# Sliding-window attention layers: the causal mask and the query lengths move from TensorE and a separate scaling pass into the VectorE pass over the scores; scaled rotary tables are kept in DRAM

## The chip, the cores and the metric

One core of one Trainium2 chip runs the whole program in one launch. The metric is the device time of an execution in microseconds, as the median of several runs. A profiled execution gives the trace that is read below; it has its own time.

## The reference

The input is x of 4 sequences of 2048 tokens with 256 features, in fp32. First comes a full attention block (16 heads of 16) with a Gaussian prior on the scores. Then come two layers of local attention and feed-forward. Only the local attention is touched in substance by the change. It computes, with windows of 128 tokens and 8 heads of 64:

```python
h = shift_token(x); q, k, v = split(h @ wqkv)      # 256 -> 3 x 512
q = q / max(|q|, 1e-12) * q_scale                  # the same for k
q, k = rotary_xpos(q, k)                           # q*cos*s + rotate_half(q)*sin*s, k with 1/s
sim = 8 * q @ k.T                                  # 128 queries by 256 keys: window before and own
sim = where((i < j) | (i > j + 128) | (j == -1), -max, sim)
x = x + (softmax(sim) @ v) @ wo
```

A length of q is one factor for each query and head, and so one factor for each row of `sim`.

## The kernel before, in words

`program` (the last function but one) runs `attention`, and then for each of two layers `local_layer` and `feed_forward`. x stays in SBUF as `xs`, 64 tiles of 128 tokens.

`local_layer` handles the 64 tiles one after another (NT = 64; each sequence has W = 16 of them). Every engine has its own written-out order, a loop over iterations n, and works in iteration n on several tiles at once: the projections of tile n, the transposes of q and k of tile n-1, the scores of tile n-2, transposes of probabilities and P V of tile n-3, and the output projection of tile n-4. Semaphores tie the engines together. The order in one iteration is:

- TensorE: `qkv` for q and k (12 matmuls of 512 columns, L1039), transpose of q (`qk_T`, L1050), `qkv` for v (6 matmuls), scores of head pair 0 (`sim`), transposes of p for pairs 0 and 1 (L1080), transpose of k, scores of pair 1, output projection (L1103, L1106), scores of pair 2, transposes of p for pairs 2 and 3, transpose of x for the next tile (L1024), scores of pair 3, P V (L1092). A `sim` is a bf16 matmul of the mask against an identity over a whole bank (L1061), which starts the bank, then two matmuls with `kh` and two with `kl` that add the scores (L1068). q and k are fp32 numbers split in a high and a low part.
- VectorE: `scale` of tile n-1 (L1265: q and k together, 1024 elements a partition, times their inverse lengths), a reciprocal, `o_lo` (L1295), `rotate` (L1242, 1024 elements), low part of q, first half of `rotate_half` (L1248), maximum of the scores of pair 0 (`sim`, L1282: one reduce for two heads, negated), second half of `rotate_half`, low part of k, maximum of pair 1, `lengths` (L1256, L1258), a reciprocal, maximum of pair 2, residual add `out` (L1303, L1305), a reciprocal, `x_lo` (L1232, the low part of the next tile's input), maximum of pair 3, a reciprocal.
- ScalarE: copies out of PSUM, squares, and the exponentials `sim` (L1181), which take the negated maximum as bias and write the sum of each row. In its order, `x_hi` (L1140), which `x_lo` needs, stands behind the exponentials of pair 2.
- GpSimd: a memset at one n in 16 (`zero_row`, L1356), `normalise` of four pairs (L1375, 512 elements each), `scale_table` (L1361: the rotary table of the next tile times q_scale and k_scale), and its part of `lengths`: the sum of the two rotation products (L1366) and the inverse lengths (L1368, a power of -0.5).
- SyncE issues the DMAs: `stack` (L1414 to L1418) moves q and k parts into place for the scores, `load_table` (L1402) fetches a table of 128 KB for every tile. For tile t of each of the 4 sequences the same 16 tables are fetched and scaled again.

The score banks are `S[0]` and `S[1]`, used alternately, so pair 2 waits for the exponentials of pair 0 and pair 3 for those of pair 1.

Of the kernel before, what the change touches and what calls it, by code (L numbers as in the profile page):

```python
# [257 lines left out]
def attention(nc, xs, x1, a):  # L258
# [297 lines left out]
    def vector(eng):  # L556
# [67 lines left out]
        def pass1(n, c):  # L624
            g, qb = divmod(n + LEAD, W)
            if g >= NB * HA:
                return
            i, k = slot["p1", g, qb, c]
            dve.wait_ge(s_full[i], k)
            o = 512 * c - 128 * qb  # L630
            if -512 - BAND < o < 128 + BAND:
                if junk_of:
                    dve.wait_ge(*junk_of.pop())
                junk_of.append((s_free[i], k))
                t = eng.tensor_tensor_reduce(junk[:, :], banks[i], gw[:, o + WIDE0:o + WIDE0 + 512], 1.0, 0.0, ALU.add, ALU.max, mx[g % 2][:, qb, c:c + 1])  # L635
            else:
                t = eng.tensor_reduce(mx[g % 2][:, qb, c:c + 1], banks[i], X, ALU.max)  # L637
            t.then_inc(s_free[i], 1)
            if (qb, c) == (W - 1, 3):
                dve.wait_ge(s_free[i], k)  # L640
                dve.wait_ge(s_dve, step.on(eng.tensor_reduce(nm[:, :], mx[g % 2][:, :, :], X, ALU.max, negate=True)))
                if g:
                    i, k = slot["rows", g - 1]
                    dve.wait_ge(s_full[i], k)
                dve.wait_ge(s_dve, step.on(eng.tensor_copy(pk[:, 0, :], nm[:, :])))
                dve.wait_ge(s_dve, step.on(eng.tensor_tensor(r1[:, :], nm[:, :], pk[:, 0, :], ALU.subtract)))
                dve.wait_ge(s_dve, step.on(eng.tensor_copy(pk[:, 1, :], r1[:, :])))
                eng.tensor_tensor(pk[:, 2, :], r1[:, :], pk[:, 1, :], ALU.subtract).then_inc(s_pk, 1)
# [264 lines left out]
NEG = -3.3895313892515355e38  # L913
# [5 lines left out]
def rotary():  # L919

    half = np.arange(0, DL, 2, dtype=np.float32)
    inv = np.float32(1.0) / np.float32(10000.0) ** (half / np.float32(DL))
    t = np.arange(L, dtype=np.float32)
    f = t[:, None] * inv[None, :]
    f = np.concatenate([f, f], 1)
    base = (half + np.float32(0.4 * DL)) / np.float32(1.4 * DL)
    power = (t - np.float32(L // 2)) / np.float32(64.0)
    s = base[None, :] ** power[:, None]
    s = np.concatenate([s, s], 1)
    sign = np.concatenate([-np.ones(32), np.ones(32)]).astype(np.float32)  # L930
# [24 lines left out]
def local_layer(nc, xs, layer, a):  # L955
# [6 lines left out]
    ident, identb = sb("ident", [128, 128]), sb("identb", [128, 128], BF16)  # L962
    mask = [sb(f"mask{i}", [128, 2, 2, 128], BF16) for i in range(2)]
# [7 lines left out]
    ss, ri = [sb(f"ss{i}", [128, 16]) for i in range(2)], [sb(f"ri{i}", [128, 16]) for i in range(2)]  # L971
# [7 lines left out]
    oT = [sb(f"oT{k}", [128, 512], F32R) for k in range(2)]  # L979
    G = [ph.ps(f"G{i}", [128, 512]) for i in range(2)]  # L980
# [31 lines left out]
    def tensor(eng):  # L1012
# [30 lines left out]
        def qk_T(t, n):  # L1043
            pe.wait_ge(s_ready, t + 1)
            if n:
                pe.wait_ge(s_ql, t + 1)
            elif t:
                pe.wait_ge(s_kl, t)
            for i in range(4):
                m = eng.transpose(T[:, i * 128:i * 128 + 128], t1[t % 2][:, n, 2 * i:2 * i + 2, :].rearrange("p h d -> p (h d)"), ident[:, :])  # L1050
            m.then_inc(s_qkT, 1)

        def sim(t, pair):
            w, s = t % W, S[pair % 2]
# [6 lines left out]
            eng.matmul(s[:, :], identb[:, :], mask[place(t, 0)][:, :, :, :].rearrange("p h k n -> p (h k n)"), start=True, stop=False, skip_group_check=True)  # L1061
# [71 lines left out]
    def scalar(eng):  # L1133
# [37 lines left out]
        def sim(t, pair):  # L1171
# [5 lines left out]
            for h in range(2):  # L1177
# [3 lines left out]
                y = eng.activation(dst, src, ACT.Exp, bias=nm[t % 2][:, hh:hh + 1], accum_out=sm[t % 2][:, hh:hh + 1])  # L1181
# [44 lines left out]
    def vector(eng):  # L1226
# [33 lines left out]
        def scale(t):  # L1260
            s = t % 2
# [3 lines left out]
            eng.tensor_tensor(flat, flat, ri[s][:, :].unsqueeze(2).to_broadcast([128, 16, DL]), ALU.mult).then_inc(s_ready, 1)  # L1265
# [12 lines left out]
        def sim(t, pair):  # L1278
# [3 lines left out]
            eng.tensor_reduce(nm[t % 2][:, 2 * pair:2 * pair + 2], s[:, :].rearrange("p (h k) -> p h k", h=2) if w else z[:, :, 1, :],  # L1282
                              X, ALU.max, negate=True).then_inc(s_max, 1)

        def recip(t, pair):
            o = 2 * pair
            dve.wait_ge(s_exp, pos(t, pair))
            if t > 1:
                dve.wait_ge(s_norm, pos(t - 2, pair))
            eng.reciprocal(rc[t % 2][:, o:o + 2], sm[t % 2][:, o:o + 2]).then_inc(s_rc, 1)  # L1290
# [30 lines left out]
        for n in range(NT + 4):  # L1321
            if n == 0:
                dve.wait_ge(s_cw, 48)
                for i in range(2):
                    for k in range(2):
                        m = eng.tensor_copy(mask[i][:, :, k, :], mask32.rearrange("p (h k n) -> p h k n", h=2, k=2)[:, :, k ^ i, :])
# [4 lines left out]
            on(recip, n - 3, 3)  # L1331
# [9 lines left out]
            on(recip, n - 2, 0)  # L1341
            on(sim, n - 2, 2)
            on(out, n - 4)
            on(recip, n - 2, 1)
            on(x_lo, n + 1)
            on(sim, n - 2, 3)
            on(recip, n - 2, 2)

    def gpsimd(eng):
# [13 lines left out]
        def lengths(t):  # L1363
# [4 lines left out]
            eng.tensor_tensor(ri[s][:, :], ss[s][:, :], nh[:, :], ALU.pow).then_inc(s_inv, 1)  # L1368

        def normalise(t, pair):  # L1370
# [3 lines left out]
            pool.wait_ge(s_rc, pos(t, pair))  # L1374
# [10 lines left out]
        for n in range(NT + 4):  # L1385
# [4 lines left out]
            on(scale_table, n + 1)  # L1390
            on(lengths, n)

    def sync(eng):
# [36 lines left out]
        load_wqkv(2)  # L1430
        for n in range(NT + 1):
# [345 lines left out]
```

## Time and profile before

| | |
|---|---|
| median of 3 runs | 6263.26 us (6263.15 to 6264.88) |
| the profiled execution's own time | 6266.61 us |
| its span | 6264.8 us |
| local layers, by the windows 3595 to 4450 and 4936 to 5792 | 855 and 856 us |
| busy in the first of them | PE 831.16, DVE 750.74, ACT 642.51, POOL 761.39 us |

PE is TensorE's matmuls, PEld its weight loads, DVE VectorE, ACT ScalarE, POOL GpSimd, SPq the queue of SyncE. A row of a timeline gives the start in us from the span's start, the duration in us, engine, line, operation, output tile <- input tiles, shape and count; "x2" is two instructions run together into one row, and a bracket at the end is idle time before it and who ended it. Starts tell more than durations here: on TensorE and VectorE an instruction starts before the record of the one ahead of it has ended, so the price of one is read from start to start.

### The profile page before, as it was taken

To read this page: it belongs to the slowest core of one execution; us is meant where nothing else is said; L and a number is where in the kernel's file an instruction comes from. 1 tells how busy PE (TensorE), PEld (TensorE's weight loads), DVE (VectorE), ACT (ScalarE), POOL (GpSimd) and SP (SyncE) were. 2 spreads that over 40 slices of the span, in tenths; PEclk is the share of its full clock that TensorE was granted. 3 is DMA by queue.
4 is the path that set the end of the run, shared out by engine and by line. 5 is a ranking of instruction groups with operands and counts; after the bars stand their busy time and mean duration, and the time that the engine had idled before them with its cause. 6 is when DMAs were issued, how large, how long until landed. Compare 5 with 4: busy or idle time off the path is not lost. (4 is left out here: it accounts for less than half of the span.)

```text
span 6264.8 us, 108066 instructions
## 1 busy us (share of the span) xinstructions
PE 5943.0 (95%) x40672; PEld 3318.7 (53%) x40672; DVE 4985.5 (80%) x10559; ACT 3827.3 (61%) x6354; POOL 1850.8 (30%) x1259
## 2 busy tenths in 40 slices
PE   6999999999998999999999799999899899999999
PEld 2333333333333333332323278888788688888788
DVE  5877888888888777888888588898666688888666
ACT  1666665666665666656666567777533477777332
POOL 3001000000000011000000089899400399989111
PEclk7999999999999999999999999999999899999999
DMA  2001101001001111001000145445300245544211
GB/s 84 23 28 35 32 16 43 27 29 31 28 20 38 33 35 35 17 30 29 17 16 16 43 108 117 112 114 114 78 11 8 67 112 117 117 113 111 61 51 44
DMA packets 264079, 338.39 MB, mean 54 GB/s; under 512 B 47324, under 2 KB 166916, under 8 KB 263556
## 3 DMA queue, kind: packets, MB, share of 16 engines
q1 hardware_dynamic: 263556, 331.48, 21.0%
q8 instruction: 321, 5.26, 0.4%
q14 instruction: 202, 1.65, 0.1%
HBM read 104.04 MB, written 41.94 MB: 23 GB/s over the span
## 5 line engine op out<-in xcount | busy, mean ns | idle before, releaser
L533 ACT ACTIVATE a_pr<-a_w 128x1024 f32<-128x1024 f32 x2048 | 2076.7, 1023 | 1150.5 <-PE a_w L421 830.1
L637 DVE TENSOR_REDUCE a_mx<-a_b 128x1 f32<-128x512 f32 x2688 | 1740.0, 685 | 327.7 <-PE a_b L405 308.5
L405 PE MATMUL a_b<-a_kp,a_qp 96*128 96x512 bf16 x4096 | 1445.6, 387 | 111.8 <-DVE a_mx L637 48.6
L421 PE MATMUL a_w<-a_qp,a_kp 99*128 99x512 bf16 x4096 | 1226.1, 380 | 33.8 <-ACT a_pr L533 33.7
L635 DVE CUSTOM_DVE_ANT_0 a_junk<-a_b,a_gw 128x512 bf16<-128x512 f32 x1408 | 965.5, 686 | 248.7 <-PE a_b L405 209.2
L452 PE MATMUL a_po<-a_pr,a_v 128*17 128x512 f32 x8192 | 1068.9, 595 | 0.5 <-ACT a_pr L533 0.5
L405 PEld LDWEIGHTS a_b<-a_kp,a_qp 96*128 96x128 bf16 x4096 | 335.4, 97 | 1255.9 <-issue 701.6
L1375 POOL TENSOR_TENSOR l_p<-l_p,l_rc 128x512 f32<-128x512 f32 (+1 forms) x512 | 725.4, 1445 | 28.7 <-DVE l_rc L1290 28.5
L421 PEld LDWEIGHTS a_w<-a_qp,a_kp 99*128 99x128 bf16 x4096 | 388.4, 98 | 521.7 <-ACT a_pr L533 110.8
L1039 PE MATMUL l_G<-l_wqkv,l_hT 128*128 128x512 f32 x2304 | 620.8, 415 | 40.4 <-DVE l_hT L1232 24.0
L746 POOL TENSOR_TENSOR a_rs<-a_ve,a_nh 128x2 f32<-128x2 f32 (+1 forms) x48 | 38.4, 800 | 2015.6 <-DVE a_ve L613 1752.5
L1181 ACT ACTIVATE l_p<-l_S,l_nm 128x256 f32<-128x256 f32 (+1 forms) x1024 | 470.6, 469 | 209.5 <-DVE l_nm L1282 209.4
L1514 PE MATMUL f_F<-f_hT,f_w 128*114 128x512 f32 x2304 | 560.5, 399 | 0.7 <-DVE f_b L1647 0.7
L1039 PEld LDWEIGHTS l_G<-l_wqkv,l_hT 128*128 128x128 f32 x2304 | 426.2, 194 | 148.9 <-DVE l_hT L1232 31.8
L756 POOL TENSOR_TENSOR a_less<-a_tmp,a_stage 128x512 f32<-128x512 f32 x64 | 74.1, 1158 | 1324.4 <-ACT a_tmp L525 880.0
L1514 PEld LDWEIGHTS f_F<-f_hT,f_w 128*114 128x114 f32 x2304 | 401.7, 177 | 120.2 <-issue 0.8
L1368 POOL TENSOR_TENSOR l_ri<-l_ss,l_nh 128x16 f32<-128x16 f32 x128 | 372.5, 2910 | 22.1 <-DVE l_ss L1258 14.3
L1366 POOL TENSOR_TENSOR l_t<-l_t 128x1024 f32<-128x1024 f32 x128 | 305.3, 2385 | 155.7 <-DVE l_t L1248 155.7
L1282 DVE TENSOR_REDUCE l_nm<-l_S 128x2 f32<-128x512 f32 (+1 forms) x512 | 338.1, 660 | 11.0 <-PE l_S L1068 10.8
L1569 ACT ACTIVATE f_u<-f_uf 114x512 fp32r<-114x512 f32 x192 | 121.4, 632 | 368.0 <-DVE f_uf L1621 368.0
L436 PEld LDWEIGHTS a_w<-a_mt,a_sel 96*32 96x32 bf16 x4864 | 111.1, 93 | 417.0 <-issue 417.0
L1189 ACT ACTIVATE l_pT<-l_R 128x512 f32<-128x512 f32 (+1 forms) x512 | 271.5, 583 | 77.4 <-PE l_R L1080 70.6
(167 smaller groups left out, 8465.6 us busy)
## 6 DMA issues: line engine op xcount, KB each, us to landing
l_qs<-l_qT SPq DMA_DIRECT2D x512, 128.0 KB, 2.3
l_kh<-l_kT SPq DMA_DIRECT2D x512, 128.0 KB, 2.4
l_kl<-l_kT SPq DMA_DIRECT2D x256, 128.0 KB, 2.4
a_qp<-q_parts SPq DMA_DIRECT2D x384, 64.0 KB, 2.2
a_kp<-k_parts SPq DMA_DIRECT2D x384, 64.0 KB, 2.2
a_xc<-in_x SPq DMA_DIRECT2D x32, 512.0 KB
l_tab<-in_rotary SPq DMA_DIRECT2D x128, 128.0 KB, 2.4
q_parts<-a_stage SPq DMA_DIRECT2D x32, 384.0 KB, 2.5
```

The lines of the kernel that those rows point to most:

```text
L405: eng.matmul(bk, qp[s][0:96, qb * 128:qb * 128 + 128], kp[s][0:96, c * 512:c * 512 + 512], start=True, stop=True).then_inc(full, 1)
L421: m = eng.matmul(wide[u][:, c * 512:c * 512 + 512], kp[s][0:99, kb * 128:kb * 128 + 128], qp[s][0:99, u * 1024 + c * 512:u * 1024 + c * 51 ...
L452: m = eng.matmul(po[32 * j:32 * j + DA + 1, :], v[b % 2][:, kb, h, :], pr[(2 * n + j // 2) % NP][:, (j % 2) * 512:(j % 2) * 512 + 512], st ...
L533: eng.activation(pr[(2 * n + u) % NP][:, :], wide[u][:, :], ACT.Exp, scale=0.25).then_inc(s_exp[u], 1)
L635: t = eng.tensor_tensor_reduce(junk[:, :], banks[i], gw[:, o + WIDE0:o + WIDE0 + 512], 1.0, 0.0, ALU.add, ALU.max, mx[g % 2][:, qb, c:c + 1])
L637: t = eng.tensor_reduce(mx[g % 2][:, qb, c:c + 1], banks[i], X, ALU.max)
L1039: m = eng.matmul(G[n % 2][:, :], hT[x][:, c * 128:c * 128 + 128], wq[z][:, c, n * 512:n * 512 + 512], start=i == 0, stop=i == 5)
L1181: y = eng.activation(dst, src, ACT.Exp, bias=nm[t % 2][:, hh:hh + 1], accum_out=sm[t % 2][:, hh:hh + 1])
L1282: eng.tensor_reduce(nm[t % 2][:, 2 * pair:2 * pair + 2], s[:, :].rearrange("p (h k) -> p h k", h=2) if w else z[:, :, 1, :], X, ALU.max, n ...
L1368: eng.tensor_tensor(ri[s][:, :], ss[s][:, :], nh[:, :], ALU.pow).then_inc(s_inv, 1)
L1375: eng.tensor_tensor(z, z, rc[t % 2][:, o:o + 2].unsqueeze(2).to_broadcast([128, 2, 256 if w else 128]), ALU.mult).then_inc(s_norm, 1)
L1514: m = eng.matmul(f[0:FW, :], w1[x][:, c, col * FW:col * FW + FW], hT[g % 2][z][:, c, :], start=n == 0, stop=n == 5)
```

## The change

The mask matmul goes, and with it the bf16 identity. The first `kh` matmul of a pair now starts the bank. The table of q is negated (factor -8), so the scores come out negated and unscaled by the length of q. VectorE's `sim` becomes two `tensor_tensor_reduce` a pair, one for each head: (score + mask) times the inverse length of q, written back in place in PSUM, with the minimum into `nm`. Its mask is 0 or a huge positive number. The exponential reads the bank with scale -1. `scale` is left with k alone (512 elements), and the transpose of q waits for the rotation instead of for `scale`. There are three `ri` buffers instead of two, with two waits on GpSimd for them. The four reciprocals of a tile become two of double width. Scaled tables are written to DRAM during the first 16 tiles of a layer (`keep_table`) and fetched from there for the other 48, for which `scale_table` is not run. In `attention` the start value of an existing `tensor_tensor_reduce` becomes the lowest number instead of 0.

```diff
 def sim(t, pair):                       # tensor
-    pe.wait_ge(s_idb, 1)
-    pe.wait_ge(s_mask, 1)
-    eng.matmul(s[:, :], identb[:, :], mask[place(t, 0)]..., start=True, stop=False, skip_group_check=True)
...
-                       start=False, stop=True, skip_group_check=True)
+                       start=x is kh and h == 0, stop=True, skip_group_check=True)

 def qk_T(t, n):                         # tensor
-    pe.wait_ge(s_ready, t + 1)
+    pe.wait_ge(s_ready if n else s_rot, t + 1)

 def scale(t):                           # vector
-    flat = t1[s][:, :, :, :].rearrange("p a h d -> p (a h) d")
-    eng.tensor_tensor(flat, flat, ri[s][:, :]....to_broadcast([128, 16, DL]), ALU.mult).then_inc(s_ready, 1)
+    k = t1[t % 2][:, 1, :, :]
+    eng.tensor_tensor(k, k, ri[t % 3][:, HL:2 * HL]....to_broadcast([128, HL, DL]), ALU.mult).then_inc(s_ready, 1)

 def sim(t, pair):                       # vector
     dve.wait_ge(s_sim, pos(t, pair))
-    eng.tensor_reduce(nm[t % 2][:, 2 * pair:2 * pair + 2], s..., X, ALU.max, negate=True).then_inc(s_max, 1)
+    dve.wait_ge(s_inv, t + 1)
+    for h in range(2):
+        hh = 2 * pair + h
+        y = s[:, h * 256:h * 256 + 256] if w else z[:, h, 1, :]
+        m = eng.tensor_tensor_reduce(y, y, mask[place(t, 0)][:, :] if w else mask[0][:, 128:256], ri[t % 3][:, hh:hh + 1], -LOWEST,
+                                     ALU.add, ALU.min, nm[t % 2][:, hh:hh + 1])
+    m.then_inc(s_max, 1)

-def recip(t, pair):                     # 2 elements; after exp of the pair
+def recip(t, half):                     # 4 elements; after exp of pair 2 * half + 1
...
 def lengths(t):                         # gpsimd
+    if t > 2:
+        pool.wait_ge(s_max, pos(t - 3, 3))
+        pool.wait_ge(s_ready, t - 2)
     eng.tensor_tensor(ri[t % 3][:, :], ss[s][:, :], nh[:, :], ALU.pow).then_inc(s_inv, 1)
...
-            on(scale_table, n + 1)
+            if n + 1 < W:
+                scale_table(n + 1)

 def load_table(t):                      # sync
+    for k in range(max(t - 3, 0), t - 2) if t < W else range(W - 3, W):
+        sp.wait_ge(s_kept[k % 3], 16 * (k // 3 + 1))
-    eng.dma_start(tab[t % 3]..., a["rotary"][:, t % W, :, :, :])...
+    eng.dma_start(tab[t % 3]..., a["rotary"][:, t, :, :, :] if t < W else scaled[t % W, :, :, :, :])...
+def keep_table(t):
+    sp.wait_ge(s_table, t + 1)
+    eng.dma_start(scaled[t, :, :, :, :], tab[t % 3]...).then_inc(s_kept[t % 3], 16)
```

In VectorE's order the reciprocal of pairs 0 and 1 stands behind the residual add, and that of pairs 2 and 3 behind `scale` of the next iteration.

## Rows read from the trace of the kernel before

**Rows 1.** The page's busy times: us, share of the span, instructions.
```profile
PE 5943.0 (95%) x40672; PEld 3318.7 (53%) x40672; DVE 4985.5 (80%) x10559; ACT 3827.3 (61%) x6354; POOL 1850.8 (30%) x1259
```
**Rows 2.** Windows: us, busy (count) of PE, PEld, DVE, ACT, POOL, clock, DMA.
```profile
5200.00:5400.00 200.00, 198.38 (x1544) 173.03 (x1546) 179.01 (x300) 154.53 (x420) 184.58 (x107) 1.00 0.51 115
```
**Rows 3.** Timeline of PE, two tile starts, a pair's scores, a later tile start.
```profile
4111.68 3.06 PE L1039 MATMUL l_G<-l_wqkv,l_hT 128*128 128x512 f32 x12
...
4124.98 3.06 PE L1039 MATMUL l_G<-l_wqkv,l_hT 128*128 128x512 f32 x12
...
4212.99 0.38 PE L1061 MATMUL l_S<-l_mask,l_identb 128*128 128x512 bf16 x1
...
4213.44 0.40 PE L1068 MATMUL l_S<-l_kl,l_qs 128*128 128x256 f32 x2
4213.68 1.08 PE L1103 MATMUL l_G<-l_wo,l_oT 128*128 128x512 f32 x4
...
4219.54 3.06 PE L1039 MATMUL l_G<-l_wqkv,l_hT 128*128 128x512 f32 x12
```
**Rows 4.** Timeline of POOL in the same stretches.
```profile
4109.11 2.91 POOL L1368 TENSOR_TENSOR l_ri<-l_ss,l_nh 128x16 f32<-128x16 f32 x1 [0.15 <-DVE l_ss L1258]
...
4122.35 2.91 POOL L1368 TENSOR_TENSOR l_ri<-l_ss,l_nh 128x16 f32<-128x16 f32 x1
...
4178.33 3.03 POOL L1375 TENSOR_TENSOR l_p<-l_p,l_rc 128x512 f32<-128x512 f32 x3
...
4206.22 6.00 POOL L1375 TENSOR_TENSOR l_p<-l_p,l_rc 128x512 f32<-128x512 f32 x4
4212.18 1.18 POOL L1361 TENSOR_TENSOR l_tab<-l_tab,l_qsc 128x256 f32<-128x256 f32 x1
4214.04 2.39 POOL L1366 TENSOR_TENSOR l_t<-l_t 128x1024 f32<-128x1024 f32 x1 [0.69 <-DVE l_t L1248]
4216.63 2.91 POOL L1368 TENSOR_TENSOR l_ri<-l_ss,l_nh 128x16 f32<-128x16 f32 x1 [0.20 <-DVE l_ss L1258]
```
**Rows 5.** Timeline of DVE in the same stretches.
```profile
4178.33 4.11 DVE L1265 TENSOR_TENSOR l_t<-l_t,l_ri 128x1024 f32<-128x1024 f32 x1
...
4206.43 1.91 DVE L1265 TENSOR_TENSOR l_t<-l_t,l_ri 128x1024 f32<-128x1024 f32 x1
...
4209.98 1.34 DVE L1242 TENSOR_TENSOR l_t<-l_qk,l_tab 128x1024 f32<-128x1024 f32 x1 [0.98 <-ACT l_qk L1148]
...
4212.69 0.68 DVE L1282 TENSOR_REDUCE l_nm<-l_S 128x2 f32<-128x512 f32 x1
...
4217.57 0.42 DVE L1305 TENSOR_TENSOR xs<-l_G,xs 128x256 f32<-128x256 f32 x1
4217.91 0.16 DVE L1290 RECIPROCAL l_rc<-l_sm 128x2 f32<-128x2 f32 x1
4218.71 0.42 DVE L1232 TENSOR_TENSOR l_hT<-l_G,l_hT 128x256 fp32r<-128x256 f32 x1 [0.64 <-ACT l_hT L1140]
```
**Rows 6.** Lines L1265 and L1248 over the span: duration ns minimum/median/maximum.
```profile
L1265 DVE TENSOR_TENSOR l_t<-l_t,l_ri x128: 1226/1985/4115, 3608.2 to 5786.4; 128x1024 f32<-128x1024 f32 x128
...
L1248 DVE TENSOR_TENSOR l_t<-l_qk,l_tab x256: 673/681/928, 3601.3 to 5780.1; 128x512 f32<-128x512 f32 x128
```
**Rows 7.** Timeline of DVE in the attention block: reduces and `tensor_tensor_reduce`, 512 wide.
```profile
1999.33 1.28 DVE L637 TENSOR_REDUCE a_mx<-a_b 128x1 f32<-128x512 f32 x2
...
2002.20 0.08 DVE L635 DVE_READ_ACCUMULATOR2_ANT a_mx<- 128x1 f32 x1
2002.43 0.69 DVE L635 CUSTOM_DVE_ANT_0 a_junk<-a_b,a_gw 128x512 bf16<-128x512 f32 x1
2003.05 0.08 DVE L635 DVE_READ_ACCUMULATOR2_ANT a_mx<- 128x1 f32 x1
2003.05 0.69 DVE L637 TENSOR_REDUCE a_mx<-a_b 128x1 f32<-128x512 f32 x1
```
**Rows 8.** Timeline of SPq: the load of a table.
```profile
4205.23 0.58 SPq L1402 DMA_DIRECT2D l_tab<-in_rotary  x1
```

More of the change, by code:

```diff
@@ L17 @@
 EPS = 1e-5
+LOWEST = -3.4028234663852886e38
 HA, DA = 16, 16
@@ L634, in pass1 @@
                 junk_of.append((s_free[i], k))
-                t = eng.tensor_tensor_reduce(junk[:, :], banks[i], gw[:, o + WIDE0:o + WIDE0 + 512], 1.0, 0.0, ALU.add, ALU.max, mx[g % 2][:, qb, c:c + 1])
+                t = eng.tensor_tensor_reduce(junk[:, :], banks[i], gw[:, o + WIDE0:o + WIDE0 + 512], 1.0, LOWEST, ALU.add, ALU.max, mx[g % 2][:, qb, c:c + 1])
             else:
@@ L912 @@
 HL, DL = 8, 64
-NEG = -3.3895313892515355e38
+FAR = 3.3895313892515355e38
 FC, FW = 6, 114
@@ L961, in local_layer @@
     qsc = sb("qsc", [128, 2, 2, DL])
-    ident, identb = sb("ident", [128, 128]), sb("identb", [128, 128], BF16)
-    mask = [sb(f"mask{i}", [128, 2, 2, 128], BF16) for i in range(2)]
+    ident = sb("ident", [128, 128])
+    mask = [sb(f"mask{i}", [128, 256], BF16) for i in range(2)]
     nh = sb("nh", [128, 16])
@@ L970, in local_layer @@
     t2 = sb("t2", [128, 2, HL, DL])
-    ss, ri = [sb(f"ss{i}", [128, 16]) for i in range(2)], [sb(f"ri{i}", [128, 16]) for i in range(2)]
+    ss, ri = [sb(f"ss{i}", [128, 16]) for i in range(2)], [sb(f"ri{i}", [128, 16]) for i in range(3)]
     qT, kT = [sb(f"qT{k}", [128, 4, 128], F32R) for k in range(2)], [sb(f"kT{k}", [128, 4, 128], F32R) for k in range(2)]
@@ L979, in local_layer @@
     oT = [sb(f"oT{k}", [128, 512], F32R) for k in range(2)]
+    scaled = nc.dram_tensor(f"scaled{layer}", [W, 128, 2, 2, DL], F32, kind="Internal").ap()
     G = [ph.ps(f"G{i}", [128, 512]) for i in range(2)]
@@ L1180, in sim @@
                 src = s[:, h * 256:h * 256 + 256] if w else z[:, h, 1, :]
-                y = eng.activation(dst, src, ACT.Exp, bias=nm[t % 2][:, hh:hh + 1], accum_out=sm[t % 2][:, hh:hh + 1])
+                y = eng.activation(dst, src, ACT.Exp, scale=-1.0, bias=nm[t % 2][:, hh:hh + 1], accum_out=sm[t % 2][:, hh:hh + 1])
             y.then_inc(s_exp, 1)
@@ L1281, in sim @@
             dve.wait_ge(s_sim, pos(t, pair))
-            eng.tensor_reduce(nm[t % 2][:, 2 * pair:2 * pair + 2], s[:, :].rearrange("p (h k) -> p h k", h=2) if w else z[:, :, 1, :],
-                              X, ALU.max, negate=True).then_inc(s_max, 1)
-        def recip(t, pair):
-            o = 2 * pair
-            dve.wait_ge(s_exp, pos(t, pair))
+            dve.wait_ge(s_inv, t + 1)
[6 more added lines that the diff above has]
+        def recip(t, half):
+            o = 4 * half
+            dve.wait_ge(s_exp, pos(t, 2 * half + 1))
             if t > 1:
-                dve.wait_ge(s_norm, pos(t - 2, pair))
-            eng.reciprocal(rc[t % 2][:, o:o + 2], sm[t % 2][:, o:o + 2]).then_inc(s_rc, 1)
+                dve.wait_ge(s_norm, pos(t - 2, 2 * half + 1))
+            eng.reciprocal(rc[t % 2][:, o:o + 4], sm[t % 2][:, o:o + 4]).then_inc(s_rc, 1)
         def o_lo(t):
@@ L1430, in sync @@
         load_wqkv(2)
+        keep_table(0)
         for n in range(NT + 1):
@@ L1439, in sync @@
                 stack(n - 1, 1)
+            if n + 1 < W:
+                keep_table(n + 1)
             if n + 2 < NT:
```

35 lines of the change are left out of this document (17 added, 18 removed).

## The prediction, made before the changed kernel was run

> **What bounds the kernel now.** I read the page's busy times first: PE is the busiest engine, at 95% [rows 1]. The windows then show that in a local layer PE is busy for 198.38 of 200 us at full clock, and that POOL (184.58) and DVE (179.01) stand close behind [rows 2]. PE's timeline gives the period: the projections of one tile start at 4111.68 and those of the next at 4124.98, 13.30 us later [rows 3]. The PE order is a solid chain with no hole worth a tenth. The two layers hold 128 such tiles.
>
> What matters is how far the next limits are. POOL's inverse lengths in the same two tiles start at 4109.11 and 4122.35, 13.24 us apart [rows 4]: POOL and DVE drift ahead of PE, by 0.06 a tile, so they turn in a loop of their own of 13.24. That loop is seen in the timelines of POOL and DVE from 4206 on [rows 4, 5]. When the power (L1368) ends, POOL begins to normalise. Three normalisations alone take 3.03 us, but four beside DVE's work take 6.00 instead of 4.0 [rows 4]. The two missing microseconds are `scale` and `rotate`: `scale` takes 1.23 when nothing stands beside it and 1.91 to 1.99 here [rows 5, 6], and `rotate` ends only once a normalisation has ended. Operations of DVE with two SBUF inputs and those of POOL take turns, whole instruction by whole instruction. So the loop is: power, two normalisations with `scale` between them, a third, `rotate`, low part, first half of the rotation, maximum 0 (4212.69), the other half, low part, maximum 1, lengths, power (4216.63, 2.91 long), normalise at 4219.5.
>
> The Trainium skill has this in "SBUF — State Buffer" (the part on ports and contention): the pair of ports that VectorE and GpSimd share is an exclusive lock for a whole instruction, taken by VectorE operations with two SBUF inputs. The 6.00 against 4.0 agrees. It also says that a pass with one input in PSUM does not take the lock, so the new passes over the scores should not be stretched.
>
> A third chain goes through `x_lo`: projections, copy of q and k, `rotate`, three maxima, the exponentials of pair 2, `x_hi`, `x_lo` (4218.71, 0.42 long), projections of the next tile at 4219.54. It has 0.41 us of air less the hand-over, so it is about 12.9 long [rows 3, 5].
>
> **PE.** The mask matmul starts at 4212.99, the `kl` pair at 4213.44 and what follows at 4213.68 [rows 3]. Two 256-column matmuls cost 0.24, `kh` the same, and the mask 0.45 - 0.24 = 0.21. Four a tile are 0.84, which leaves PE a floor of 13.30 - 0.84 = 12.46. The bounds of one are 0.16 (the first `kh` weights no longer load behind the mask) and 0.23. If PE alone counted, the layers would win 0.84 x 128 = 108 us. It does not: the loop of 13.24 takes over after 0.06.
>
> **DVE, `scale`.** 512 elements instead of 1024. Alone the sizes take 1.23 and 0.68 [rows 6], so 0.55 less, both on DVE and in the time POOL stands still. This is in the POOL loop. It is not in the `x_lo` chain: DVE is idle for 0.98 before `rotate`, until ACT's copy [rows 5].
>
> **DVE, the scores.** One reduce has a start-to-start price of 0.60 (two are 1.28, the last 0.68) [rows 7]. Two passes of 256 replace it. The nearest row for 256 elements out of PSUM is the residual add: 4217.57 to 4217.91, 0.34 [rows 5]. Two are 0.68, so a pair costs d = +0.08. Each pass also carries a read of its accumulator. A reduce behind it starts in the same instant (both 2003.05), but another such pass starts 0.23 after the read (2002.20 to 2002.43); there a semaphore for the junk buffer lies between [rows 7], which the new code does not have. So d lies between +0.08 and 0.34 + 0.23 + 0.34 - 0.60 = +0.31, and if the gap follows both passes, at +0.54. Below 0.08 I see nothing. Writing back to PSUM in place has no row, nor the factor read per partition; the residual add reads PSUM and writes SBUF, and so does the attention pass; 512 against 256 elements (0.60 against 0.34) is 1.0 ns an element. I take d = 0.12, nearest to the add, with something for the read in the middle.
>
> The Trainium skill speaks against splitting here: "VectorE: DVE Perf Modes", section "The DRAIN you can't avoid", has the next operation start only once the pipe is empty, and a fixed 151 cycles beside one cycle an element. By that rule two passes of 256 are 0.85 against 0.69, d = +0.16. The rows show starts 0.08 before the end of the one ahead; by the rule instead of the rows the total would be some 10 us higher than mine.
>
> **The loops after.** POOL loop: 13.24 - 0.55 + 2d (maxima 0 and 1 lie in it; maximum 2 does not) = 12.69 + 2d = 12.93. `x_lo` chain: 12.9, less a reciprocal moved out from ahead of maximum 2 (0.08), plus 3d, less 0.1 to 0.2 because PE brings the transposes of p earlier and ACT, which stands between maxima 1 and 2, no longer waits for them: 13.0 to 13.1. PE: 12.46. I take a period of 13.0: 0.30 less, in 128 tiles 38.4 us.
>
> **The slip.** One tile in 16 has a memset ahead of the normalisation. `scale` and the normalisation then start together (both 4178.33), POOL wins three times, and `scale` takes 4.11 [rows 4, 5]. That is 2.1 over its usual 1.99, of which the idle 0.98 covers most of one microsecond: 1.2 lost. After the change the third normalisation needs the reciprocal that stands behind `scale` on DVE, so `scale` starves behind two at most: 2.0 + 0.7 = 2.7, covered by the idle time. It happened six times: 7.2 us.
>
> **What costs nothing, and why.** `scale_table` (1.18) goes from 48 tiles in 64, but POOL waits 0.69 for DVE right behind it [rows 4]: the wait becomes 1.9. POOL busy falls by about 1.1 x 96 = 100 us, and the time by nothing; it would count only if POOL were loaded without gaps. Two of four reciprocals go, 0.08 each from start to start: one is the 0.08 above, the other lies ahead of idle time. The transpose of q no longer waits for `scale`; PE gets to it some 2.9 into the tile, so this is air. POOL's two new waits stand ahead of the power, on maxima and a `scale` more than a tile old; behind them only the normalisations queue. DVE's new wait for the inverse lengths is for a tile whose power ended a period earlier. SP: `keep_table` waits for a table that POOL has scaled at 4213.4, halfway in its tile, and SP gets there at about 4205.23, a microsecond before the next tile starts on PE [rows 8]; behind it stand only a table two tiles ahead and the next `stack`, over six microseconds later. One issue of 0.6 fits. Once a layer, ahead of table 16, SP waits for a 128 KB store to land, some 2 to 3 us, inside the same gap. 32 stores in all. The start value in attention is another constant: nothing. With PE at 12.4 of 13.0 I expect its clock to stay at 2.4 GHz in the layers; the rows of before cannot show it.
>
> **Sum.** The profiled execution took 6266.6. 6266.6 - 38.4 - 7.2 = 6221.0. The median shown is 3.3 below that execution, so 6217.7, as 6218.
>
> **Rivals.**
> - *The accumulator gap is real.* With d = 0.31 the POOL loop is 13.31 and the `x_lo` chain 13.3 to 13.5: the period is what it was, only the slip pays, 6256 to 6270. For it: the 0.23 in [rows 7]. Against: a self-wait explains part of it.
> - *DVE's passes become the bound and the kernel slows.* If each pass pays its gap, or reading and writing one PSUM bank in place is slower than the add, d reaches 0.54: the loop is 13.77, 0.47 over 13.30, in 128 tiles +60, less 7: 6316. In between, d = 0.40 gives 13.49, +24 - 7 = 6280. The point is d = 0.30, where 12.69 + 2d passes 13.30. For it: DVE and POOL were 0.06 from binding already, so almost nothing has to go wrong. Against: no row shows a pass of DVE over PSUM that takes more than that 1.0 ns an element.
> - *The locks fall well.* If, with `scale` short, `rotate` finds POOL idle, another microsecond leaves the loop, and PE's floor binds: 6266.6 - 108 - 7 - 3 = 6148. Against: four normalisations and half a `scale` need 4.6 us from the power's end and `rotate` starts 3.7 into the tile; they must meet.
> - *It doesn't do what it says*, for instance tables from DRAM come late: the load is issued two tiles ahead, so hardly.
>
> **How the numbers follow.** Forecast (d from 0.08 to 0.22, period 12.85 to 13.13, 6200 to 6236) 0.57; partial gap and accumulator gap, 6236 to 6275, 0.20; slower by over 0.2%, 0.17; PE's floor 0.05; the last 0.01. About 0.2% (12.5 us) is what a measurement of this kernel tells from no change. Faster by more (below 6250.8): 0.57 + 0.05 + 0.05 of the partial gap = 0.67. Same: 0.14. Slower (above 6275.8): 0.19 with the tail of the gap case. The range for 8 in 10 leaves out most of the PE floor and the upper half of the slower cases: 6188 to 6284.
>
> **What would show it.** PE: no L1061, its floor visible as idle time of about 0.5 a tile. Starts of L1368 12.9 to 13.1 apart. `scale` near 1.3 to 1.5 us and POOL's four normalisations 5.5 instead of 6.0. Two custom passes whose starts lie 0.34 to 0.38 apart; 0.57 would be the gap. POOL waiting about 1.9 ahead of L1366 from tile 16 on. No `scale` of 4 us. The prediction is wrong if the pair costs over 0.90, or if `rotate` no longer meets a normalisation.

## The result, and the profile after

| | before | after |
|---|---|---|
| median | 6263.2 us (4 runs) | 6310.66 us (4 runs, 6308.54 to 6311.41) |
| the profiled execution | 6266.61 us | 6308.54 us |

The ratio is 1.0076, with a 95% interval of 1.0058 to 1.0093: slower, by 47 us. The forecast was 6218.

The windows of the same stretch as [rows 2] show that PE did give up its load (188.74 of 200 us busy instead of 198.38), and POOL too (139.46 instead of 184.58). DVE's share is about the same.

```profile
5200.00:5400.00 200.00, 188.74 (x1423) 160.56 (x1422) 176.91 (x433) 151.85 (x408) 139.46 (x89) 1.00 0.46 109
```

PE's timeline has the next tile's projections 13.88 after those of the last (4217.46 to 4231.34; 13.30 before, [rows 3]). Now they wait for `x_lo` (L1231). The `kh` matmuls of a pair start at 4222.20, `kl` at 4222.44 and what follows at 4222.67, so 0.47 instead of the 0.69 from 4212.99 to 4213.68 in [rows 3]: the mask's 0.22 is saved in full.

```profile
4217.46 3.07 PE L1041 MATMUL l_G<-l_wqkv,l_hT 128*128 128x512 f32 x12 [0.24 <-DVE l_hT L1231]
...
4222.20 0.39 PE L1067 MATMUL l_S<-l_kh,l_qs 128*128 128x256 f32 x2
4222.44 0.40 PE L1067 MATMUL l_S<-l_kl,l_qs 128*128 128x256 f32 x2
4222.67 1.04 PE L1079 MATMUL l_R<-l_ident,l_p 128*128 128x128 f32 x8
...
4231.34 1.90 PE L1041 MATMUL l_G<-l_wqkv,l_hT 128*128 128x512 f32 x7 [0.23 <-DVE l_hT L1231]
```

DVE's timeline of that tile answers to [rows 5]:

```profile
4218.13 1.18 DVE L1266 TENSOR_TENSOR l_t<-l_t,l_ri 128x512 f32<-128x512 f32 x1
...
4221.20 2.09 DVE L1244 TENSOR_TENSOR l_t<-l_qk,l_tab 128x1024 f32<-128x1024 f32 x1 [0.66 <-ACT l_qk L1147]
...
4224.41 0.48 DVE L1287 CUSTOM_DVE_ANT_0 l_S<-l_S,l_mask,l_ri 128x256 f32<-128x256 f32 x1
4224.81 0.14 DVE L1287 DVE_READ_ACCUMULATOR2_ANT l_nm<- 128x1 f32 x1
4224.81 0.48 DVE L1287 CUSTOM_DVE_ANT_0 l_S<-l_S,l_mask,l_ri 128x256 f32<-128x256 f32 x1
4225.22 0.14 DVE L1287 DVE_READ_ACCUMULATOR2_ANT l_nm<- 128x1 f32 x1
4225.22 0.68 DVE L1250 TENSOR_TENSOR l_t<-l_qk,l_tab 128x512 f32<-128x512 f32 x1
```

Two things are to be seen. A pair costs 0.81 from start to start (4224.41 to 4225.22), so d = 0.81 - 0.60 = 0.21; the forecast took 0.12. And `rotate` lasts 2.09 instead of 1.34. POOL's timeline says why (the first row is a window that begins inside the four normalisations, so it holds the last two):

```profile
4220.17 2.04 POOL L1381 TENSOR_TENSOR l_p<-l_p,l_rc 128x512 f32<-128x512 f32 x2
...
4217.73 4.48 POOL L1381 TENSOR_TENSOR l_p<-l_p,l_rc 128x512 f32<-128x512 f32 x4
4225.98 2.38 POOL L1369 TENSOR_TENSOR l_t<-l_t 128x1024 f32<-128x1024 f32 x1 [3.77 <-DVE l_t L1250]
4228.73 2.91 POOL L1374 TENSOR_TENSOR l_ri<-l_ss,l_nh 128x16 f32<-128x16 f32 x1 [0.36 <-DVE l_ss L1260]
```

The last two normalisations take 2.04 from 4220.17, so the last one starts at about 4221.17, and `rotate` asks at 4221.20. It loses by 0.03 and stands until POOL is done at 4222.21; it ends 1.08 after that. In the kernel before, `rotate` asked while the third was running (4209.98, the third from 4209.20 to 4210.23) and went ahead of the last. Over all tiles the median of `rotate` went from 1459 to 2094 ns:

```profile
L1244 DVE TENSOR_TENSOR l_t<-l_qk,l_tab x128: 1224/2094/2099, 3593.4 to 5820.9; 128x1024 f32<-128x1024 f32 x128
```

### The profile page after: what moved, and what is told of

Same layout as the page of the kernel before. It is cut to its first block and busy times, and to the rows that moved or that the text cites. A ratio compares the mean times of both kernels' runs of the same rounds, so it can differ in the third digit from the quotient of the medians.

```text
span 6306.8 us, 108286 instructions
## 1 busy us (share of the span) xinstructions
PE 5905.7 (94%) x40160; PEld 3257.2 (52%) x40160; DVE 5022.6 (80%) x11837; ACT 3843.6 (61%) x6354; POOL 1588.6 (25%) x1163
## 5 line engine op out<-in xcount | busy, mean ns | idle before, releaser
L1381 POOL TENSOR_TENSOR l_p<-l_p,l_rc 128x512 f32<-128x512 f32 (+1 forms) x512 | 562.2, 1126 | 23.6 <-DVE l_rc L1296 23.2
L1287 DVE CUSTOM_DVE_ANT_0 l_S<-l_S,l_mask,l_ri 128x256 f32<-128x256 f32 (+1 forms) x1024 | 444.9, 474 | 7.5 <-PE l_S L1067 7.4
L1244 DVE TENSOR_TENSOR l_t<-l_qk,l_tab 128x1024 f32<-128x1024 f32 x128 | 252.6, 1973 | 93.7 <-ACT l_qk L1147 92.9
```

Source lines behind the costliest of these rows:

```text
L1287: m = eng.tensor_tensor_reduce(y, y, mask[place(t, 0)][:, :] if w else mask[0][:, 128:256], ri[t % 3][:, hh:hh + 1], -LOWEST, ALU.add, ALU ...
L1381: eng.tensor_tensor(z, z, rc[t % 2][:, o:o + 2].unsqueeze(2).to_broadcast([128, 2, 256 if w else 128]), ALU.mult).then_inc(s_norm, 1)
```

## The experiments

Each starts from the changed kernel, or where it says so from the kernel before. Medians are of 4 or 10 executions (e6 has one), the ratio is to the kernel before, executed beside them. Periods are read from the starts of the projections on PE. Theory A, in what was expected, is that the order in which `rotate` and the last normalisation get the lock sets the period; theory B, that the longer passes over the scores do it alone.

**e1: the last normalisation after `rotate`.**

```diff
             for pair in range(4):
+                if pair == 3 and n < NT:
+                    pool.wait_ge(s_turn, n + 1)      # incremented by rotate(n)
                 on(normalise, n - 3, pair)
```

> The changed kernel; only edit: POOL normalises pair 3 of tile n-3 only after DVE's rotate of tile n. Theory A (the shared lock: with the half-size scale, normalisation 3 starts in the same instant as rotate, 4221.20, and rotate runs 2.10 instead of 1.34): rotate goes back to about 1.35; normalisation 3 then meets the first rotate_half instead, so maximum 0 starts some 0.35 earlier in the tile, period 13.5 instead of 13.88, about 6265 us. Theory B (the longer passes over the scores alone set the period, the lock is incidental): period stays within 0.1 of 13.88, 6300 to 6315.

Measured: 6273.98 us, ratio 1.0014 (1.0005 to 1.0024). DVE's, POOL's and PE's timelines:

```profile
4212.26 1.23 DVE L1244 TENSOR_TENSOR l_t<-l_qk,l_tab 128x1024 f32<-128x1024 f32 x1 [0.66 <-ACT l_qk L1147]
...
4214.01 1.15 DVE L1250 TENSOR_TENSOR l_t<-l_qk,l_tab 128x512 f32<-128x512 f32 x1
```
```profile
4213.57 1.04 POOL L1381 TENSOR_TENSOR l_p<-l_p,l_rc 128x512 f32<-128x512 f32 x1 [1.29 <-DVE l_t L1244]
```
```profile
4208.53 3.06 PE L1041 MATMUL l_G<-l_wqkv,l_hT 128*128 128x512 f32 x12 [0.24 <-DVE l_hT L1231]
...
4222.02 3.07 PE L1041 MATMUL l_G<-l_wqkv,l_hT 128*128 128x512 f32 x12 [0.23 <-DVE l_hT L1231]
```

One added wait on an engine with air takes 37 us off. `rotate` is back at 1.23, the normalisation now meets the first `rotate_half` (1.15 instead of 0.68), and the period is 13.49, as theory A had it.

**e2: the last normalisation after the first `rotate_half`.** As e1, but the semaphore is incremented by `rotate_half(n, 0)`.

> The changed kernel; only edit: POOL normalises pair 3 of tile n-3 only after the first rotate_half of tile n. Theory A: rotate about 1.25 to 1.35 and the first rotate_half 0.68, maximum 0 about 0.75 earlier in the tile; the second rotate_half may wait up to 0.3 for normalisation 3; period 13.1 to 13.3, 6210 to 6240. Theory B: unchanged or slower, because POOL now waits more: 6300 to 6330.

Measured: 6256.75 us, ratio 0.9986 (0.9977 to 0.9996). The tile starts are 13.28 apart:

```profile
4206.32 3.07 PE L1041 MATMUL l_G<-l_wqkv,l_hT 128*128 128x512 f32 x12 [0.24 <-DVE l_hT L1231]
...
4219.60 3.07 PE L1041 MATMUL l_G<-l_wqkv,l_hT 128*128 128x512 f32 x12 [0.24 <-DVE l_hT L1231]
```

`rotate` and the first `rotate_half` are free now, and the second `rotate_half` is held for 0.26:

```profile
4210.06 1.23 DVE L1244 TENSOR_TENSOR l_t<-l_qk,l_tab 128x1024 f32<-128x1024 f32 x1 [0.66 <-ACT l_qk L1147]
...
4213.21 0.94 DVE L1250 TENSOR_TENSOR l_t<-l_qk,l_tab 128x512 f32<-128x512 f32 x1
```

The period is inside what theory A gave, the total 17 us above it. Part of that, some 5 us, is that the first 15 tiles of a layer, in which POOL still scales tables, ran at 13.50; I had not reckoned with them. The rest was not looked into.

**e3: `scale` on 1024 elements again.** The length of q is applied twice.

```diff
-            k = t1[t % 2][:, 1, :, :]
-            eng.tensor_tensor(k, k, ri[t % 3][:, HL:2 * HL]...)
+            k = t1[t % 2][:, :, :, :].rearrange("p a h d -> p (a h) d")
+            eng.tensor_tensor(k, k, ri[t % 3][:, :]...)
...
-            pe.wait_ge(s_ready if n else s_rot, t + 1)
+            pe.wait_ge(s_ready, t + 1)
```

> The changed kernel, with scale on 1024 elements again (q and k), and the transpose of q waiting for it as before; the length of q is then applied twice, so the scores are not the reference's. Theory A: 0.5 us more of DVE work a tile pushes normalisation 3 behind rotate, rotate 1.4 to 1.6, period 13.65, about 6282: faster than the changed kernel with more work on the engine. Theory B: DVE has 0.5 to 0.7 more a tile, period 13.9 to 14.4, 6312 to 6375.

Measured: 6298.25 us, ratio 1.0054 (1.0039 to 1.0069). DVE does more and the kernel is 12 us faster than the changed one. The two ratios alone hardly tell that from nothing; the tile starts do, 13.67 apart instead of 13.88. `rotate` takes 1.62, and the first `rotate_half` 0.93:

```profile
4207.85 0.93 DVE L1250 TENSOR_TENSOR l_t<-l_qk,l_tab 128x512 f32<-128x512 f32 x1
...
4216.30 1.71 DVE L1266 TENSOR_TENSOR l_t<-l_t,l_ri 128x1024 f32<-128x1024 f32 x1
...
4219.37 1.62 DVE L1244 TENSOR_TENSOR l_t<-l_qk,l_tab 128x1024 f32<-128x1024 f32 x1 [0.66 <-ACT l_qk L1147]
```

The sign and the period (13.67) are theory A's; the total is 16 us above its number.

**e4: the kernel before without the mask matmul**, the first `kh` matmul starting the bank, nothing in its place.

```diff
-            eng.matmul(s[:, :], identb[:, :], mask[place(t, 0)]..., start=True, stop=False, skip_group_check=True)
...
-                                   start=False, stop=True, skip_group_check=True)
+                                   start=x is kh and h == 0, stop=True, skip_group_check=True)
```

> The kernel before without the mask matmul and nothing in its place (the softmax runs over all 256 keys). Theory A, with the loop of POOL and DVE at 13.24: period 13.2 to 13.25, 6250 to 6257. Rival (PE alone bounds the kernel before): period 12.46, about 6155.

Measured: 6256.18 us, ratio 0.9985 (0.9976 to 0.9995). Tile starts are 13.25 apart:

```profile
4214.63 3.07 PE L1039 MATMUL l_G<-l_wqkv,l_hT 128*128 128x512 f32 x12
...
4227.88 3.06 PE L1039 MATMUL l_G<-l_wqkv,l_hT 128*128 128x512 f32 x12
```

So of PE's 0.84 only 0.05 a tile was to be had: the loop of 13.24 read from [rows 4] is real.

**e5: one pass of 512 for two heads**, with the factor and the minimum of one head for both; the first window of a sequence keeps two.

```diff
-            for h in range(2):
+            for h in range(1 if w else 2):
                 hh = 2 * pair + h
-                y = s[:, h * 256:h * 256 + 256] if w else z[:, h, 1, :]
+                y = s[:, :] if w else z[:, h, 1, :]              # the mask tile is 512 wide
```

> The changed kernel with one pass of 512 for the two heads of a pair instead of two of 256 (both heads then share the factor and the minimum of one head; the first window of a sequence keeps two passes), so the output is not the reference's. In the changed kernel the pair costs 0.81 from start to start, 0.21 over the reduce. Theory A (price and lock together): one pass costs 0.60 to 0.66, the cost over the reduce falls to about 0.05; the chain through x_lo gets 0.45 to 0.5 shorter, so tiles start earlier against POOL, normalisation 3 comes behind rotate again (rotate 1.3 to 1.8); period 12.9 to 13.2, 6210 to 6245. Rival (the price counts, the lock doesn't flip): period 13.88 - 0.48 = 13.4, about 6255 to 6265, rotate still 2.1.

Measured: 6201.19 us, ratio 0.9897 (0.9880 to 0.9913). From start to start the pass is 0.67 (d = 0.07), and `rotate` is held in 6 of 128 tiles only:

```profile
4213.39 1.23 DVE L1244 TENSOR_TENSOR l_t<-l_qk,l_tab 128x1024 f32<-128x1024 f32 x1 [0.80 <-ACT l_qk L1147]
...
4215.99 0.75 DVE L1287 CUSTOM_DVE_ANT_0 l_S<-l_S,l_mask,l_ri 128x512 f32<-128x512 f32 x1
4216.66 0.14 DVE L1287 DVE_READ_ACCUMULATOR2_ANT l_nm<- 128x1 f32 x1
4216.66 0.68 DVE L1250 TENSOR_TENSOR l_t<-l_qk,l_tab 128x512 f32<-128x512 f32 x1
```

The period is 12.86, and it and the time are even just below theory A's ranges. 0.14 less a pair took 1.02 off the tile; the price alone, in three or four pairs, would have taken 0.4 to 0.6.

**e6: the factor as the constant 1.0** in the passes; the lengths of q are left out.

```diff
-                m = eng.tensor_tensor_reduce(y, y, mask..., ri[t % 3][:, hh:hh + 1], -LOWEST,
+                m = eng.tensor_tensor_reduce(y, y, mask..., 1.0, -LOWEST,
```

> The changed kernel with the factor of the passes over the scores as the constant 1.0 instead of the inverse length of q (left out, so the scores are too large). One look at a pass's price, 0.40 from start to start and 0.48 long against 0.34 and 0.42 of the residual add of the same size. If the factor read per partition is the surplus: 0.34 to 0.36 and 0.42. If it is the write back to PSUM or the accumulator read: 0.40 as before, and the period 13.88.

Measured: 6216.53 us in one execution. A pair is 0.72 (4219.72 to 4220.44, d = 0.12), and `rotate` isn't held:

```profile
4217.13 1.22 DVE L1244 TENSOR_TENSOR l_t<-l_qk,l_tab 128x1024 f32<-128x1024 f32 x1 [0.74 <-ACT l_qk L1147]
...
4218.87 0.93 DVE L1250 TENSOR_TENSOR l_t<-l_qk,l_tab 128x512 f32<-128x512 f32 x1
4219.72 0.42 DVE L1287 CUSTOM_DVE_ANT_0 l_S<-l_S,l_mask 128x256 f32<-128x256 f32 x1
4220.06 0.14 DVE L1287 DVE_READ_ACCUMULATOR2_ANT l_nm<- 128x1 f32 x1
4220.06 0.46 DVE L1287 CUSTOM_DVE_ANT_0 l_S<-l_S,l_mask 128x256 f32<-128x256 f32 x1
4220.44 0.14 DVE L1287 DVE_READ_ACCUMULATOR2_ANT l_nm<- 128x1 f32 x1
4220.44 0.68 DVE L1250 TENSOR_TENSOR l_t<-l_qk,l_tab 128x512 f32<-128x512 f32 x1
```

The factor read per partition is the surplus: without it the first pass is 0.34, exactly the residual add. The second is 0.38; I put its 0.04 down to the read of the accumulator ahead of it, which no run separates. This kernel has, by accident, the d of the forecast, and it has the period of the forecast: 13.02 against 13.0. Its one execution took 6216.5 us, against 6221.0 in the forecast's sum for a profiled execution. The 0.09 a pair between it and the changed kernel are worth 0.86 a tile.

**e7: the passes write to SBUF.** In this cut `d` is the tile that is written, and not the price d.

```diff
+            if t > 1:
+                dve.wait_ge(s_pT, 4 * (t - 2) + pair + 1)        # the p tile has been read
...
-                m = eng.tensor_tensor_reduce(y, y, mask...
+                m = eng.tensor_tensor_reduce(d, y, mask...       # d: this head's rows of the p tile
...
-                y = eng.activation(dst, src, ACT.Exp, scale=-1.0, ...
+                y = eng.activation(dst, dst, ACT.Exp, scale=-1.0, ...
```

> The changed kernel with the passes writing to the p tile in SBUF, where the exponential works in place, instead of back into the score bank. If the write to PSUM is the surplus of 0.06 a pass: 0.34 to 0.36 from start to start, six passes in the x_lo chain give 0.35, period about 13.5. If it isn't: 0.40, and the period moves only by what the exponentials cost out of SBUF (0.47 from start to end now): 13.8 to 14.2.

Measured: 6312.61 us, ratio 1.0075 (1.0060 to 1.0090). The passes still start 0.40 and 0.41 apart, and the period is 13.88. The write back in place costs nothing:

```profile
4213.71 0.47 DVE L1290 CUSTOM_DVE_ANT_0 l_p<-l_S,l_mask,l_ri 128x256 f32<-128x256 f32 x1
4214.11 0.08 DVE L1290 DVE_READ_ACCUMULATOR2_ANT l_nm<- 128x1 f32 x1
4214.11 0.47 DVE L1290 CUSTOM_DVE_ANT_0 l_p<-l_S,l_mask,l_ri 128x256 f32<-128x256 f32 x1
```

**e8: the kept tables alone, in the kernel before** (the hunks of `scale_table`, `load_table`, `keep_table` and `rotate` of the change, nothing else).

> The kernel before with one part of the change alone: scaled tables kept in DRAM, scale_table run for 16 tiles of 64. All theories: POOL busy 100 us less, the first rotate_half 0.68 instead of 0.92 from tile 16 on, period still 13.29 because PE sets it: 6260 to 6268. A gain of over 10 us would mean that POOL's load as such mattered.

Measured: 6259.39 us, ratio 0.9991 (0.9981 to 1.0000), period still 13.29, and POOL busy 101 us less in the windows of the two layers. That is 6 us at most. One part of what was expected did not come: the first `rotate_half` stays at 0.92. So in this kernel it is the last normalisation that holds it, and not `scale_table`.

**e9: a mask matmul back in the changed kernel**, its result overwritten by the next.

```diff
+            eng.matmul(s[:, :]..., mask[0][:, 0:128], mask[0][:, :].unsqueeze(1).to_broadcast([128, 2, 256]), start=True, stop=False, ...)
             pe.wait_ge(s_qs[t % 2], 64 * (t // 2 + 1))
```

> The changed kernel with a bf16 matmul of 512 columns back in front of the kh matmuls of every pair, whose result the next matmul overwrites. Theory A (DVE, POOL and ACT set the period of 13.88, PE has air): PE is busy 0.84 more a tile, period 13.85 to 14.0, 6305 to 6325. If PE's saving still counts in the changed kernel: 13.88 + 0.84, about 6415.

Measured: 6315.69 us, ratio 1.0083 (1.0067 to 1.0098). The windows show PE at 196.00 of 200, and the tile starts are still 13.89 apart. In the changed kernel PE's saving bought 5 us at most. The two ratios don't tell that from nothing; the tile starts show 3 us of it, in six intervals where a sequence begins, 13.43 with the mask matmul instead of 12.90.

```profile
4000.00:4200.00 200.00, 196.00 (x1481) 165.28 (x1478) 176.00 (x431) 150.32 (x405) 140.97 (x90) 1.00 0.46 109
...
4207.55 3.07 PE L1041 MATMUL l_G<-l_wqkv,l_hT 128*128 128x512 f32 x12
...
4221.44 3.06 PE L1041 MATMUL l_G<-l_wqkv,l_hT 128*128 128x512 f32 x12
```

**e10: the next tile's input earlier.** Three moves of one call each:

```diff
 # tensor
             on(sim, n - 2, 1)
+            on(x_T, n + 1)
             on(out, n - 4)
 # scalar
             on(sim, n - 2, 0)
+            on(x_hi, n + 1)
             on(sim, n - 2, 1)
 # vector
             on(sim, n - 2, 2)
+            on(x_lo, n + 1)
             on(out, n - 4)
             on(recip, n - 2, 0)
```

> The changed kernel with one edit: the chain for the next tile's input is moved up. TensorE transposes x right after the scores of pair 1, ScalarE copies it (x_hi) between the exponentials of pairs 0 and 1, VectorE makes x_lo ahead of the residual add. The third maximum and its exponentials then no longer stand before the next tile's projections. Theory A: PE starts tiles earlier against POOL, so normalisation 3 comes behind rotate again and the POOL loop rules: period 13.1 to 13.4, 6215 to 6250. Rival (the order of the locks stays, rotate still waits for all four normalisations): 13.6 to 13.88, 6275 to 6310.

Measured: 6221.47 us, ratio 0.9932 (0.9918 to 0.9947): better than both kernels, the same computation as the changed one. The period is 13.13, and `rotate` goes ahead of the last normalisation again (1.40, 1.39). DVE now waits 0.24 for POOL's power, which shows the POOL loop ruling:

```profile
4205.53 1.40 DVE L1244 TENSOR_TENSOR l_t<-l_qk,l_tab 128x1024 f32<-128x1024 f32 x1 [0.92 <-ACT l_qk L1147]
...
4215.63 1.45 DVE L1266 TENSOR_TENSOR l_t<-l_t,l_ri 128x512 f32<-128x512 f32 x1 [0.24 <-POOL l_ri L1374]
...
4218.67 1.39 DVE L1244 TENSOR_TENSOR l_t<-l_qk,l_tab 128x1024 f32<-128x1024 f32 x1 [0.92 <-ACT l_qk L1147]
```

**e11: e10 and e2 together.**

> e10's edit and e2's (normalisation 3 after the first rotate_half) together. Theory A: the POOL loop in e2 was at its edge (third normalisation ended 0.03 before rotate), so the period stays 13.2 to 13.3 although the x_lo chain is gone: 6230 to 6255. If the x_lo chain was all that held e2: 12.6 to 12.8, 6175 to 6200.

Measured: 6231.7 us, ratio 0.9947 (0.9930 to 0.9963), period 13.14 once the tables are off POOL and 13.36 before. The time is in theory A's range, the period just below its 13.2 to 13.3. The turn adds nothing where the order of the locks is already right; while tables are scaled it costs 0.2 a tile.

**e12: e10, and normalisations 2 and 3 after the first `rotate_half`** (e2's wait at `pair == 2`).

> e10's edit, and normalisations 2 and 3 both after the first rotate_half of the next tile. Theory A: only two normalisations and scale stand before rotate (2.5 instead of 3.5 from the power's end), the second rotate_half waits for one of them; the POOL loop falls by up to 1.0 and the exponentials of pair 1 and PE's floor come next: period 12.6 to 12.9, 6175 to 6210, below both kernels. Rival (two normalisations in the middle block the second rotate_half by a microsecond and delay the power): 13.2 or more, 6240 and up.

Measured: 6224.97 us, ratio 0.9938 (0.9923 to 0.9953). A miss: 12.97 from tile 16 on, above the 12.6 to 12.9, and 13.45 in the 15 tiles in which POOL also scales a table. POOL's timeline has hardly a gap (0.1) from the third normalisation to the power, so what was taken from ahead of `rotate` came back ahead of the power:

```profile
4210.92 2.49 POOL L1380 TENSOR_TENSOR l_p<-l_p,l_rc 128x512 f32<-128x512 f32 x2 [2.67 <-DVE l_t L1250]
4213.37 2.37 POOL L1368 TENSOR_TENSOR l_t<-l_t 128x1024 f32<-128x1024 f32 x1
4215.85 2.91 POOL L1373 TENSOR_TENSOR l_ri<-l_ss,l_nh 128x16 f32<-128x16 f32 x1
```

## Why the prediction was wrong

The sign and the size are wrong; most of the steps stand, and two failed.

*What bounds the kernel before: right.* e4 took PE's mask away alone and got 13.25, the loop of 13.24, not PE's floor.

*The step "The scores", d = 0.12: mis-sized.* It measured 0.21, inside the bounds of 0.08 and 0.31 and above the value taken. e6 splits the surplus: 0.06 in the first pass and 0.03 in the second is the factor read per partition; 0.04 is left, which I put down to the accumulator read ahead of the second. The accumulator gap of 0.23 of the first rival didn't come: without the wait for the junk buffer it is nearly nothing. The write back in place, which I named with the factor as unknown, is free (e7). By the rule that I set against my value (the Trainium skill, "VectorE: DVE Perf Modes", section "The DRAIN you can't avoid"; the 151 cycles stand in that page's section "The TRN2 errata", for an fp32 `tensor_tensor`), the estimate was 0.85 for the pair and 0.16 for d; it cost 0.81 against a reduce of 0.60. That rule, taken for the size, would have been nearer than my value, but e6 shows that it was nearer for another reason: with a constant the same two passes cost 0.72.

*The step "The loops after", as a sum linear in d: this is what failed.* With d = 0.21 my own formulas give 12.69 + 0.42 = 13.11 for the POOL loop and 12.9 - 0.08 + 0.63 - 0.15 = 13.30 for the `x_lo` chain. Both are met where the locks fall well: e10, with the `x_lo` chain out of the way, has 13.13, and e2, with POOL's turn fixed by hand, has 13.28. (The 12.9 held lock waits: `rotate` 1.34 and a first `rotate_half` of 0.92. e2 has one of about that size left, 0.26 in the second `rotate_half`.) So 0.3 of the 0.88 between 13.88 and the forecast's 13.0 is the size of d. The prediction used the second formula for its chosen d alone. It took the band up to d = 0.22 and the point of d = 0.30, from which on the kernel slows, from the POOL loop; the `x_lo` chain passes 13.30 at d = 0.21 already, and is at 13.6 for the d = 0.31 of the first rival, which has 13.3 to 13.5.

The other 0.60 a tile is the lock: `rotate` stands behind a fourth normalisation, 2.09 instead of e2's 1.23, less the 0.26 by which e2's second `rotate_half` is held. The prediction had seen the lock, and even wrote that four normalisations and half a `scale` need 4.6 us while `rotate` asks at 3.7. It used that only to say that `rotate` must meet one. It did not ask which one, and that has a point at which it decides: halving `scale` brings the last normalisation forward by 0.53, from 3.95 to 3.42 after the power's end. `rotate` asks 3.74 after the tile's start on PE. If the power ends more than 0.32 after that start, `rotate` goes first; if less, it waits a whole normalisation. In the changed kernel it ends 0.30 after. A longer chain through the maxima and `x_lo` makes PE start tiles later against POOL's power and so pushes towards "less". At d = 0.12 (e6) the kernel settles on the good side, at 0.21 on the bad one, by 0.03, so the point lies near d = 0.18 (an estimate from the two).

Neither of the two signs of being wrong that the prediction named showed: the pair cost less than 0.90, and `rotate` still met a normalisation.

The rows allow a check. Free of the lock, `rotate` takes 1.23 and a `rotate_half` 0.68. e2's period less its one wait is 13.28 - 0.26 = 13.02. If passes and lock waits of DVE ahead of `x_lo` are all that differs, the periods follow from 13.02 by adding the waits and three times what a pair costs less:

| kernel | `rotate` asks, from the power's end | `rotate` held | a `rotate_half` held | three pairs | sum | measured |
|---|---|---|---|---|---|---|
| changed | 3.44 | 0.86 | 0 | 0 | 13.88 | 13.88 |
| e1 | 3.44 | 0 | 0.47 | 0 | 13.49 | 13.49 |
| e3 | 3.44 | 0.39 | 0.25 | 0 | 13.66 | 13.67 |
| e6 | 3.36 | 0 | 0.25 | -0.27 | 13.00 | 13.02 |
| e5 | 3.31 | 0 | 0.25 | -0.42 | 12.85 | 12.86 |

The last normalisation is ready at 3.42 (in e3 at 3.95; in e1 it is held back by its new wait). In e10, whose chain is another one, `rotate` asks at 3.14. The sums are bookkeeping: they leave nothing over for another cause. That the order decides is shown by who asks first, and by the runs that turn it.

Six runs bear this out, from four sides: a wait for POOL (e1: 13.49, e2: 13.28), more work on DVE (e3: 13.67), an earlier start of tiles with all passes as they are (e10: 13.13), and cheaper passes (e5, e6: 12.86, 13.02).

*The rival that came true in sign* was "DVE's passes become the bound", with its point at d = 0.30. Slower it was, but at d = 0.21 and not by that mechanism: with passes of the same price and the locks in order, the kernel is 0.1% faster than before (e2).

*PE's price: right* (0.22 a mask, 0.21 forecast), and its saving is worth 5 us at most in the changed kernel (e9). *Tables: right* (e8, at most 6 us by themselves); that they cost nothing holds only while another wait covers them, as the 13.50 against 13.28 in e2 shows. *The slip: it goes, as forecast.* The tile that took 14.80, 1.5 over its neighbours where the forecast had 1.2, takes 13.58, less than its neighbours. `scale` stands behind two normalisations there (2.32 long at 3970.73; 2.7 was forecast) and the third waits for the reciprocal behind `scale`. So the last one would start 3.86 after the power's end, and `rotate`, which asks at 3973.79, goes first.

The sum of what happened, from the tile starts on PE: the 63 intervals of a layer add up to 842.9 before and 868.5 after in the first layer, 25.6 more, and to 25.4 more in the second. The profiled executions differ by 41.9; the rest, about 9 us less, lies outside these intervals, half of it ahead of the first layer, and was not looked into. The first tile starts at 3583.1 in the changed kernel's trace and at 3585.9 to 3589.1 in those of its variants, so that half is spread between executions. What holds e12 at 12.97 is open as well.

## What to carry to other kernels

Where two engines take turns at something whole instruction by instruction, find the instant at which each asks, and how far apart these are; a change that moves one of them past the other costs or gives a whole instruction, whatever its own size. Loops that close within half a percent of the bound are to be written down with what sets their phase, not only with their length. If an engine has air, a wait that fixes the order (e2: 0.60 of 13.88 a tile) or an order of work that removes the dependence (e10: 0.75) can give as much as cheaper instructions (e6: 0.86), most of whose gain was the order too; if a part of a saving lies on the engine with the bound, check first (as e4 does) how much of it there is to be had.

## What the runs showed of the hardware

- Behind a custom pass with a factor read per partition the next instruction starts 0.40 us later for 256 elements out of PSUM, with a constant 0.34 (e6). That it writes to PSUM or to SBUF made no difference (0.40 both), only the accumulator read behind it is recorded as 0.14 instead of 0.08.
- Two such passes in a row need hardly a gap for the accumulator read: 0.38 to 0.41 to the next. The 0.23 of [rows 7] stand where a semaphore is waited for between them; e7, whose passes write to SBUF as those do, has no such gap. The wait was not tested by itself.
- Such a pass, with its scores in PSUM, wasn't held by POOL: in the changed kernel it is 0.40 from start to start also at 4217.73, where POOL's first normalisation begins.
- While a sum of POOL runs, a 16-element operation of DVE with a single source out of SBUF ends 0.03 us behind the sum. It is held for over 0.1 us so in 120 of 128 tiles of e12 (0.69 in most, instead of 0.17), in 26 of e2 and e11, in 12 of the kernel before and in 4 of the changed one:

```profile
4215.08 0.69 DVE L1259 TENSOR_SCALAR l_ss<-l_ss 128x16 f32<-128x16 f32 x1
```

The Trainium skill ("SBUF — State Buffer", section "Who interferes with whom") has VectorE operations in a mode that uses both ports take the same exclusive lock, and names `tensor_scalar` among those that can enter it; this row agrees with it, with 0.52 us of waiting. That the operation ran in such a mode no row shows.
